# Loading the second layout of x: 32 small transfers with at most three in flight, in place of four large ones queued at once

## The reference, cut to what matters

```python
q = jnp.transpose(x, (2, 0, 1))                       # l, n, c
scores = jnp.einsum('lnc,lmc->lnm', q, q) / c ** 0.5  # 512 matrices of 32 x 32
prob = jax.nn.softmax(scores, axis=-1)
msg = jnp.einsum('lnm,lmc->lnc', prob, q)
x = layernorm(x + (x + transpose(msg, (1, 2, 0))))
# then cross attention with ctx_4096 (8 heads), and a gated FFN whose
# weights and activations are quantized in groups of 32
```

## Time and profile before

| | |
|---|---|
| median of 3 runs | 670.32 us (669.27 to 671.2) |
| profiled execution, its own time | 670.21 us |
| its span, first to last instruction | 668.4 us |
| PE busy | 607.3 us, 91% |
| DVE busy | 558.9 us, 84% |
| ACT busy | 474.1 us, 71% |
| POOL busy | 479.0 us, 72% |
| mean granted TensorE clock | 0.967 of full |

### The profile page before, as it was taken

How to read it: one execution, slowest core, us unless ns; L and a number is a source line. 1 busy time by engine, 2 the same in 40 slices (tenths; PEclk the granted TensorE clock), 3 DMA queues, 4 the chain that set the end, 5 groups by cost and what they waited for, 6 DMA issues and landing times. The chain is left out here.

```text
span 668.4 us, 13138 instructions
## 1 busy us (share of the span) xinstructions
PE 607.3 (91%) x4855; PEld 333.8 (50%) x4864; DVE 558.9 (84%) x801; ACT 474.1 (71%) x871; POOL 479.0 (72%) x634
## 2 busy tenths in 40 slices
PE   0638999899999999999999999999999979999993
PEld 0638988444545445445545445445454534444441
DVE  2757999799999999999899879898788369999992
ACT  3208665788989989888988879888888735443535
POOL 1431778769889998998888686786778544776673
PEclk9956999899999999999999999999999989999998
DMA  8993032000001011110101000000000003345645
GB/s 315 173 212 113 2 111 62 11 17 25 1 19 53 10 32 40 41 41 25 40 13 45 1 23 17 7 17 16 1 1 1 9 8 60 76 94 99 134 103 132
DMA packets 62463, 36.76 MB, mean 55 GB/s; under 512 B 44736, under 2 KB 52928, under 8 KB 62400
## 3 DMA queue, kind: packets, MB, share of 16 engines
q1 hardware_dynamic: 62400, 35.93, 22.8%
HBM read 21.82 MB, written 4.19 MB: 39 GB/s over the span
## 5 line engine op out<-in xcount | busy, mean ns | idle before, releaser
L1932 ACT ACTIVATE big<-banks 128x512 f32<-128x512 f32 x288 | 158.7, 601 | 22.3 <-PE banks L2912 9.1
L663 POOL TENSOR_TENSOR big<-big 128x512 f32<-128x512 f32 x128 | 132.3, 1062 | 21.2 <-DVE big L1187 21.1
L1164 DVE TENSOR_REDUCE big<-banks 128x1 f32<-128x512 f32 x128 | 83.0, 679 | 21.9 <-PE banks L2879 21.7
L1993 ACT ACTIVATE big<-banks,big 128x512 f32<-128x512 f32 x128 | 88.0, 694 | 18.0 <-DVE big L1164 16.8
L655 POOL TENSOR_TENSOR big<-big 128x512 f32<-128x512 f32 x64 | 82.2, 1290 | 10.1 <-ACT big L1998 9.9
L1170 DVE TENSOR_REDUCE big<-banks 128x16 f32<-128x1024 f32 x64 | 77.1, 1205 | 4.9 <-PE banks L2889 4.8
L1175 DVE TENSOR_TENSOR big<-banks,big 128x1024 f32<-128x1024 f32 x64 | 78.3, 1223 | 2.7 <-PE banks L2922 0.7
L2912 PEld LDWEIGHTS banks<-ident,big 128*128 128x128 f32 x512 | 56.6, 142 | 47.2 <-issue 22.4
L2922 PEld LDWEIGHTS banks<-ident,big 128*128 128x128 f32 x512 | 55.2, 141 | 46.6 <-issue 22.7
L2912 PE MATMUL banks<-ident,big 128*128 128x128 f32 x512 | 74.2, 281 | 2.6 <-ACT big L1993 1.5
L1998 ACT ACTIVATE big<-big 128x1024 f32<-128x1024 f32 x64 | 68.1, 1065 | 10.2 <-DVE big L1175 9.7
(11 more groups left out here) (108 smaller groups left out, 1118.6 us busy)
## 6 DMA issues: line engine op xcount, KB each, us to landing
big<-in_x_dram SPq DMA_DIRECT2D x8, 1024.0 KB, 13.7
big<-in_ctx_dram SPq DMA_DIRECT2D x16, 256.0 KB, 2.7
out_dram<-big SPq DMA_DIRECT2D x16, 256.0 KB, 2.3
big<-in_L_ffn_w_down_dram SPq DMA_DIRECT2D x4, 688.0 KB, 10.2
big<-in_L_ffn_w_gate_dram SPq DMA_DIRECT2D x10, 256.0 KB, 3.0
big<-in_L_ffn_w_up_dram SPq DMA_DIRECT2D x10, 256.0 KB, 2.9
big<-big SPq DMA_TRANSPOSE x48, 2.7
wg_area<-in_L_xattn_Wq_dram SPq DMA_DIRECT2D x2, 128.0 KB, 10.8
```

The lines of the kernel that those rows point to most:

```text
L663: pool.tensor_tensor(e, e, r, ALU.mult).then_inc(s.p_ready, 1)
L1164: dve.tensor_reduce(kneg[:, par, i:i + 1], bank[par], X, ALU.max, negate=True).then_inc(s.k_max_ready, 1)
L1932: return act.activation(dst, src, ACT.Copy)
L1993: act.activation(EK[:, f % 2, par, i], bank[par], ACT.Exp, bias=kneg[:, par, i:i + 1], accum_out=ksum[:, f % 2, par, i:i + 1]).then_inc(s. ...
```

## The change

`load_xq` is cut by 8 channels (`CQ`) as well as by the four groups of positions: 32 transfers of 128 KB, each 32 partitions x 8 channels x 128 positions, the rows of 512 bytes as before. They use three semaphores in turn, and from the fourth on SP waits, before it issues transfer n, until transfer n - 3 has landed. PE waits for all three semaphores where it waited for one.

```diff
         s.x_loaded = [sem(f"x_loaded_{piece}") for piece in range(4)]
-        s.xq_loaded = sem("xq_loaded")
+        s.xq_loaded = [sem(f"xq_loaded_{turn}") for turn in range(3)]
...
-            def load_xq(j):
-                sp.dma_start(xq[B * j:B * j + B], x[:, :, LG * j:LG * j + LG]).then_inc(s.xq_loaded, 16)
+            def load_xq(n):
+                c, j = CQ * (n // 4), n % 4
+                if n >= 3:
+                    sp.wait_ge(s.xq_loaded[n % 3], 16 * (n // 3))
+                sp.dma_start(xq[B * j:B * j + B, c:c + CQ], x[:, c:c + CQ, LG * j:LG * j + LG]).then_inc(s.xq_loaded[n % 3], 16)
...
             load_small()
-            load_xq(0)
-            load_xq(1)
-            load_xq(2)
-            load_xq(3)
+            for n in range(4 * C // CQ):
+                load_xq(n)
             load_aw(1)
...
                 if c == 0 and h == 0:
-                    pe.wait_ge(s.xq_loaded, 64)
+                    for turn in range(3):
+                        pe.wait_ge(s.xq_loaded[turn], 16 * len(range(turn, 4 * C // CQ, 3)))
```

More of the change, by code:

```diff
@@ L58, in decoder_kernel @@
     CL = 16
+    CQ = 8
     CHUNKS = LG // CL
```

## The result

| | before | changed |
|---|---|---|
| median of 20 runs each | 670.86 us | 667.27 us |
| lowest to highest | 668.69 to 673.63 | 664.51 to 669.85 |
| profiled execution | 670.21 us | 668.47 us |

The ratio is 0.9948, with a 95% interval of 0.9935 to 0.9961: 3.6 us less, where 663.5 us, 6.7 less, was predicted. 667.27 us lies outside the range that the prediction gave, 661 to 666.5.

A forecast was written before the change was run, and what follows sets the result against it. PE was taken to lack instructions beside the loads before the messages. Holes of 7.3 us (five of 1.0, one of 2.30) for 14.0 gain 6.7, so 670.2 - 6.7 = 663.5 us; range 661 to 666.5, chance 0.5.

The forecast's parts named there:

- What bounds the kernel: Before the messages PE runs out of instructions, 14.0 us of holes, as fetches come late beside loads; the rest just shifts.
- The fetch beside the new stream: PE's instruction fetch during the `xq` load takes 4.9 us, leaving holes of 1.0 us at five block boundaries.
- Rival B: Fetch latency beside the `xq` load depends on load, not queue depth: no change, 670 to 673 us; chance 0.12.
- C: Rival: fetches become free, PE's holes vanish except under large loads; gain about 10 us, 660.2 us; chance 0.12.
- The round trip: On SP, each 128 KB transfer lands 3.3 us after issue; with three in flight, 1.1 us a transfer.
- rival A: Small transfers too slow at 1.5 us each, so DVE waits for `aw(1)`: slower, 674.2 us; chance 0.12.
- Can DVE keep up?: Before the messages, DVE's 29.1 us of work fits the new 36.8 us stretch, so it does not limit the gain.
- crawling: DVE's subtraction slows beside score bursts, 3.64 us for 0.69; the resulting limit on the gain was put at 7 us.

The follow-up runs named there:

- e1: The changed kernel's 32 transfers of 128 KB, all queued at once with no wait between them; 665.48 us, ratio 0.9919 to the kernel before.
- e8: The changed kernel without SP's wait and with the load in 8 pieces of 512 KB; 670.80 us, ratio 0.9974 to the kernel before.
- e11: The kernel before with rows of x and its swapped copy 2096 bytes apart, the messages' add in four instructions; 666.69 us, ratio 0.9919.
- e13: The changed kernel without SP's wait, with rows of x and its swapped copy 2096 bytes apart; 659.45 us, ratio 0.9811 to the kernel before.
- e4: The changed kernel with both operands of the score matmuls read from neighbouring elements, giving other scores; 662.58 us, ratio 0.9874 to the kernel before.
- e2: The kernel before, its four large transfers each issued only when the one ahead had landed; 668.27 us, ratio 0.9957 to the kernel before.

## Why the prediction was wrong

**What bounds the kernel: right, and incomplete.** The holes were missing instructions, they were tied to the loads, and all that follows 66 us is carried along.

**The fetch beside the new stream: right in kind, too dear.** I took holes of 1.0 us at five boundaries and one of 2.30, 7.3 us in all. There was one, of 0.82. Rival B (the depth does not matter) is refuted by e1 against e8: the same rows of 512 bytes, engines saturated in both, no hole against 12.8 us. C (no holes) is what came, without its 10 us of gain. This error ran against the next one: with holes of 0.8 us and all else as predicted, the sum would have given 657 us. That the forecast missed its range by only 0.8 us is in part luck.

**The round trip: right.** 0.97 us a transfer for 1.1; rival A did not come.

**"Can DVE keep up?": the step that failed.** I compared sums: 29.1 us of DVE's work in 36.8 us. That supposes that DVE works while PE does. The row that says otherwise was on the table, 3.64 us for 0.69, and was read as crawling, to bound only a larger gain; for ACT and POOL it was not considered at all. (Its bound was also mis-added: 12.5 less four times 1.5 is 6.5, a little under the 6.7 that the sum takes, and not 7.) What the runs showed in its place: during a burst DVE, ACT and POOL nearly stand. The work of a chunk between one burst and the next (subtraction, exp, sum, normalising, transposing) must then be done in time in which PE does not run scores, and PE's holes had been that time. Take one hole away and PE waits for DVE or ACT instead. The stretch of the changed kernel, from 25.24 to 66.87, is made up of PE's own 29.9 us, 0.8 of issue, 7.2 for DVE and 3.7 for ACT; the prediction had the last two at nothing. So of some 13 us of holes removed, 10.9 came back as other waits.

**What is shown of the cause.** The chain stands in the changed kernel's rows: exp, held from 29.26 to 33.07, is what the sum at 33.11 waits for; the subtraction of 34.66 follows it, and PE's burst of 35.41 waits for that. In e11 to e13, where nobody is held, PE waits between its first scores and the messages for instructions and loads alone. While the others were held, 13.2 us fewer of holes gave 3.6 us, and e1, with none, 5.5 by its medians; with the rows padded, 8.5 us fewer (22.6 in e11, 14.1 in e13) gave 7.2. And padding alone, with all its holes, gives 0.9919.

**What is not shown.** Every kernel that frees the other engines also has shorter bursts of PE (2.4 us in place of 3.9), so how much of the gain is due to which was not separated. Open too is which part of the memory or of its ports two such reads share with the other engines, and why both operands are needed.

## What to carry to other kernels

Before adding up what an engine has to do in a stretch, look at the same instruction's duration beside each of its neighbours: if it ends when another engine's burst ends, the two are in series, and an idle hole of one may be the working time of the other. Holes put down to nothing, one per 256 instructions, with a packet on the instruction queue in each, call for a shorter queue of loads; here smaller transfers were enough, and a wait for their landing added nothing. Where a matmul steps by the pitch of a row, a few unused elements behind each row are worth trying before anything is reordered around it: 12 of them, with nothing else changed, gave no less here (0.9919) than the change did (0.9948).

## What the hardware showed that was not expected

- Matmuls of 32 x 32 whose weights and moving operand both step by 2048 bytes hold DVE, ACT and POOL for most of the burst (DVE's subtraction 0.69 us becomes 3.0 to 3.6, its transpose 0.7 becomes 5.4, ACT's exp 0.6 becomes 3.8 to 4.0), and run at 3.92 us per 128 themselves. At steps of 2096 bytes the 128 take 2.43 us, at 1984 bytes 2.31, with neighbouring elements 1.93, and nobody is held up. With only one operand at 2048 it is 2.56 and 2.61 us, and nobody is held up either. DVE's maximum straight out of PSUM was not held up even before the change (0.69 us at 49.10); it writes 16 elements a partition. ACT's copies out of PSUM, which write 256, are held (L1948, two of them 5.26 us at 58.23, and 0.66 in e13).
- With the wide steps the time of a burst did not depend on TensorE's granted clock: before the change 3.92 us both at 1.00 (20.57) and at 0.50 (37.03), at 2096 bytes 2.44 and 2.43 (e11). With neighbouring elements it did: 1.93 us at 0.50 and 1.30 at 1.00 (e4, 34.77 and 29.94).
- A fetch of PE's instructions beside a saturated DMA was hidden in a burst pair of 8.28 us in e1, and took 10.6 us from block to block with up to 4 MB queued; with the loads done it took 4.0 (e11). The Trainium skill (DMA: Bandwidth & Descriptors, Queues, rings and completion order) has each DMA engine take turns between its queues by packets. By that rule what else is queued would not matter; e2 against the kernel before does not agree, since the pieces are the same and holes and time from issue to landing both fall with what is queued (14.0 to 10.9 us, 16.4 to 8.0 us).
- SP's issue of a 128 KB piece in e1 took 0.45 us (median, the longest 1.64) and 0.62 on average (19.88 us for 32), a little less than the 0.73 us that the engines need to move it at 180 GB/s, so that only some 8 pieces were under way at a time (the estimate given at e1).
